# A ternary feed-forward stage with its weights made inside the attention stage before it, and its token tiles written out

## The reference

```python
def _weight_quant(w):
    scale = 1.0 / jnp.clip(jnp.mean(jnp.abs(w)), 1e-05)
    return jnp.clip(jnp.round(w * scale), -1.0, 1.0) / scale

def _act_quant(x):                      # one scale per token
    scale = 127.0 / jnp.clip(jnp.max(jnp.abs(x), axis=-1, keepdims=True), 1e-05)
    return jnp.clip(jnp.round(x * scale), -128.0, 127.0) / scale

def _bitlinear(x, w):
    return jnp.einsum('bsi,oi->bso', _act_quant(x), _weight_quant(w))

gate = silu(_bitlinear(x, w_gate))      # 256 -> 1024
up = _bitlinear(x, w_up)                # 256 -> 1024
y = _bitlinear(gate * up, w_down)       # 1024 -> 256
```

## Time and profile before

| | us |
|---|---|
| median of 3 runs | 4549.73 |
| lowest and highest | 4539.75 and 4550.23 |
| profiled execution | 4542.93 |
| its span, first to last instruction | 4541.1 |

### The profile page before, as it was taken

One profiled execution on the slowest core, in us unless ns is written; L12 is line 12 of the kernel. 1 busy time (PEld: TensorE's weight loads), 2 busy tenths in 40 slices (PEclk: granted clock), 3 DMA queues, 4 the chain that ended last, 5 costly groups with the idle time before them and its releaser, 6 DMA issues. The chain is left out here.

```text
span 4541.1 us, 74932 instructions
## 1 busy us (share of the span) xinstructions
PE 3993.9 (88%) x27065; PEld 2110.3 (46%) x27065; DVE 2500.5 (55%) x3505; ACT 1915.5 (42%) x3522; POOL 1473.1 (32%) x1327
## 2 busy tenths in 40 slices
PE   6667974969999999999999999999999999988564
PEld 4333431635554455445554455435554455435332
DVE  3583444548842688238852588228862588325522
ACT  3344534536532455326542366315643355314321
POOL 0000000026630566116640466106640366200044
PEclk8898996989999999999999999999999999998776
DMA  3000000021120111101120111101120111100386
GB/s 111 28 0 21 0 19 9 2 79 29 28 67 1 32 28 26 57 16 29 28 69 1 28 29 27 58 13 28 29 54 19 25 28 29 61 19 11 97 237 199
DMA packets 103426, 190.31 MB, mean 42 GB/s; under 512 B 14084, under 2 KB 54656, under 8 KB 101888
## 3 DMA queue, kind: packets, MB, share of 16 engines
q1 hardware_dynamic: 94832, 173.21, 13.3%
q0 software_dynamic: 6144, 9.44, 1.1%
q10 hardware_dynamic: 2064, 2.62, 0.2%
HBM read 116.38 MB, written 20.09 MB: 30 GB/s over the span
## 5 line engine op out<-in xcount | busy, mean ns | idle before, releaser
L1510 PE MATMUL PS<-locw,X 128*128 128x512 f32 x2304 | 1109.4, 610 | 81.7 <-issue 42.7
L1777 POOL TENSOR_TENSOR locm<-locm 128x512 f32<-128x512 f32 x384 | 487.7, 1270 | 1004.3 <-DVE locm L1714 1003.9
L1510 PEld LDWEIGHTS PS<-locw,X 128*128 128x128 f32 x2304 | 400.7, 193 | 533.3 <-issue 371.8
L1889 PE MATMUL PS<-locxn,locw 128*114 128x512 f32 (+1 forms) x1152 | 501.4, 593 | 13.0 <-DVE loch L1998 13.0
L1783 POOL TENSOR_TENSOR locm<-locm,locrn 128x512 f32<-128x512 f32 x384 | 392.4, 1043 | 130.2 <-ACT locrn L1629 130.2
L1790 POOL TENSOR_TENSOR locpr<-locpr,locrs 128x512 f32<-128x512 f32 x384 | 391.0, 1039 | 126.2 <-DVE locrs L1743 105.9
L1712 DVE TENSOR_TENSOR locm<-PS,loctab 128x512 f32<-128x512 f32 x384 | 263.5, 686 | 282.0 <-ACT locsq L1619 282.0
L1889 PEld LDWEIGHTS PS<-locxn,locw 128*114 128x114 f32 (+1 forms) x1152 | 204.2, 178 | 306.0 <-issue 282.9
L1654 ACT ACTIVATE locpr<-locpr 128x1024 f32<-128x1024 f32 x192 | 203.1, 1058 | 291.2 <-DVE locpr L1734 291.2
L1650 ACT ACTIVATE locpt<-PS 128x512 f32<-128x512 f32 x384 | 208.4, 595 | 263.2 <-PE PS L1520 263.2
L1998 DVE SCALAR_TENSOR_TENSOR loch<-PS,locvec,locgl 114x512 f32<-114x512 f32 x144 | 107.0, 750 | 376.4 <-PE PS L1889 327.3
(11 more groups left out here) (317 smaller groups left out, 6204.7 us busy)
## 6 DMA issues: line engine op xcount, KB each, us to landing
locve<-locva SPq DMA_DIRECT2D x372, 128.0 KB, 2.2
locw<-in_L2f_wqkv SPq DMA_DIRECT2D x42, 512.0 KB, 9.7
BIG<-in_L3f_gu SPq DMA_DIRECT2D x24, 768.0 KB
BIG<-in_L3f_down SPq DMA_DIRECT2D x24, 384.0 KB
moe_sums<-none SPq DMA_DIRECT2D x2, 4352.0 KB, 23.2
moeroom<-moe_sums SPq DMA_DIRECT2D x16, 512.0 KB, 7.0
locw<-in_L2f_w SPq DMA_DIRECT2D x6, 1364.0 KB
loctab<-in_L2f_tabs SPq DMA_DIRECT2D x7, 1024.0 KB, 10.9
```

The source lines that it names most:

```text
L1510: mm = pe.matmul(PS[:, o % 2, :], k.X[:, j, at - j:at - j + P], W[:, j, col:col + G], start=j == 0, stop=j == KD - 1)
L1777: pool.tensor_tensor(M1[:, j, :], M1[:, j, :], M2[:, x, :], ALU.add).then_inc(s.paired, 1)
L1889: mm = pe.matmul(PS[0:r, 4 + 2 * (m % 2) + half, :], W1[:, c, half * FI + m * FR:half * FI + m * FR + r], XNL[:, g % 2, c, :], start=c == ...
```

## The change

**Weights.** `stage_xattn` takes a triple of hooks, given for L0x alone. SP issues the three 1 MB loads behind the loads of the cross-attention, into unused parts of BIG. DVE does the three sums of absolute values, one each in its steps 3, 4 and 5, and the reciprocal of the means in step 7. POOL, behind its copies, adds the sums over the partitions with an all-reduce, forms the means, and does the nine passes. Five semaphores more belong to L0x. The first block of L0f is gone.

**Tiles.** The 16 tiles are written out, most tiles have two buffers, and XN is read by TensorE directly. x is quantised for two tiles at once, in DVE's odd steps, with the rounding on ACT. gate, up, silu and `hidden` go in two halves of 512 columns. The rounding of h (one pass over 1024 columns) and both products of factors go to POOL; DVE keeps maximum, scale, reciprocal and clipping. The clipping of h comes a step later, its transposes and copy two, the down product three, y's transposes and addition four.

```diff
+def bitnet_weights(k, io):
...
+    WF = [k.BIG[:, KD * T + i * 2048:KD * T + (i + 1) * 2048] for i in range(3)]
...
+    def quantise(pool):
...
+        pool.wait_ge(s.sums, 3)
+        link(pool.partition_all_reduce(k.bit_sum[:, 3:6], k.bit_sum[:, 0:3], P, RSUM))
+        link(pool.tensor_scalar(k.bit_mean[:, :], k.bit_sum[:, 3:6], 1.0 / (D * FF), 1e-5, ALU.mult, ALU.max))
+        pool.sem_inc(s.mean, 1)
+        pool.wait_ge(s.scale, 1)
+        for i in range(3):
+            link(pool.tensor_scalar(WF[i], WF[i], k.bit_scale[:, i:i + 1], ROUND, ALU.mult, ALU.add))
+            link(pool.tensor_scalar(WF[i], WF[i], ROUND, 1.0, ALU.subtract, ALU.min))
+            link(pool.tensor_scalar(k.bit_wq[i], WF[i], -1.0, None, ALU.max))
+
+    def measure(dve, n):
+        if 3 <= n < 6:
+            i = n - 3
+            dve.wait_ge(s.loaded, 48)
+            dve.tensor_reduce(k.bit_sum[:, i:i + 1], WF[i], AX.X, ALU.add, apply_absolute_value=True).then_inc(s.sums, 1)
+        if n == 7:
+            dve.wait_ge(s.mean, 1)
+            dve.reciprocal(k.bit_scale[:, :], k.bit_mean[:, :]).then_inc(s.scale, 1)
...
                 for n in range(NT + 1):
                     if n + 1 < NT:
                         shift(n + 1)
+                    if beside:
+                        beside[2](dve, n)
                     for slot in "AB":
...
+                def gate_up(n, j):
+                    m, i = divmod(n, 2)
+                    pe.wait_ge(s.xqc, m + 1)
+                    if n:
+                        pe.wait_ge(s.h, 2 * (n - 1) + j + 1)
...
+                def turn_y(n):
+                    pe.wait_ge(s.y, n + 1)
...
+                turn_x(0)
+                turn_xq(0)
+                turn_x(1)
+                for n in range(NT + 4):
+                    if n >= 4:
+                        turn_y(n - 4)
+                    if n < NT:
+                        gate_up(n, 0)
+                        gate_up(n, 1)
+                    if 2 <= n < NT + 2:
+                        turn_h(n - 2)
+                    if n % 2 == 0 and n // 2 + 1 < MX:
+                        turn_xq(n // 2 + 1)
+                    if n % 2 and n // 2 + 2 < MX:
+                        turn_x(n // 2 + 2)
+                    if 3 <= n < NT + 3:
+                        down(n - 3)
...
+                def raise_h(n):
+                    pool.wait_ge(s.h_scaled, n + 1)
+                    if n >= 2:
+                        pool.wait_ge(s.hq, n - 1)
+                    pool.tensor_scalar(HR[:, n % 2, :], H[:, n % 2, :, :].rearrange("p j n -> p (j n)"), HS[:, 2, n:n + 1], ROUND,
+                                       ALU.mult, ALU.add).then_inc(s.hr, 1)
+                    pool.tensor_scalar(HS[:, 3, n:n + 1], HS[:, 1, n:n + 1], k.bit_mean[:, 2:3], None, ALU.mult).then_inc(s.h_factor, 1)
...
+                for n in range(NT):
+                    raise_h(n)
+                    if n % 2 and n // 2 + 2 < MX:
+                        factors(n // 2 + 2)
...
+                def raise_x(m):
+                    act.wait_ge(s.x_scaled, m + 1)
+                    if m:
+                        act.wait_ge(s.xq, m)
+                    for i in range(2):
+                        act.activation(XR[:, i, :], PS[:, 4, i * D:(i + 1) * D], ACT.Copy, scale=XS[:, 2, 2 * m + i:2 * m + i + 1],
+                                       bias=ROUND).then_inc(s.xr, 1)
...
+                raise_x(0)
+                copy_xq(0)
+                raise_x(1)
+                for n in range(NT + 3):
+                    if n < NT:
+                        silu(n, 0)
+                        silu(n, 1)
+                    if 2 <= n < NT + 2:
+                        copy_h(n - 2)
+                    if n % 2 == 0 and n // 2 + 1 < MX:
+                        copy_xq(n // 2 + 1)
+                    if n % 2 and n // 2 + 2 < MX:
+                        raise_x(n // 2 + 2)
+                    if n >= 3:
+                        weigh(n - 3)
...
+                def clip_h(n):
+                    dve.wait_ge(s.hr, n + 1)
+                    if n >= 2:
+                        dve.wait_ge(s.hqt, n - 1)
+                    dve.tensor_scalar(HQ[:, n % 2, :], HR[:, n % 2, :], ROUND, 127.0, ALU.subtract, ALU.min).then_inc(s.hq, 1)
...
+                measure_x(0)
+                clip_x(0)
+                measure_x(1)
+                clip_x(1)
+                for n in range(NT + 4):
+                    if n >= 4:
+                        add(n - 4)
+                    if n < NT:
+                        hidden(n, 0)
+                        hidden(n, 1)
+                    if 1 <= n <= NT:
+                        clip_h(n - 1)
+                    if n < NT:
+                        measure_h(n)
+                    if n % 2 and n // 2 + 2 < MX:
+                        measure_x(n // 2 + 2)
+                        clip_x(n // 2 + 2)
```

More of the change, by code:

```diff
@@ new lines, in stage_bitnet_ffn @@
+def stage_bitnet_ffn(nc, k, io):
+    PS, sem = k.PS, k.sem
+    s = Names()
+    (
+        s.xt, s.x_step, s.x_scaled, s.x_factors, s.xr, s.xq, s.xqt, s.xqc, s.gate_ps, s.up_ps, s.silu, s.h, s.h_step, s.h_scaled, s.h_factor,
+        s.hr, s.hq, s.hqt, s.hqc, s.y_ps, s.y, s.yt, s.added
+    ) = (sem("bit_" + n) for n in (
+        "xt", "x_step", "x_scaled", "x_factors", "xr", "xq", "xqt", "xqc", "gate_ps", "up_ps", "silu", "h", "h_step", "h_scaled", "h_factor",
+        "hr", "hq", "hqt", "hqc", "y_ps", "y", "yt", "added"
+    ))
+    NT = T // P
+    MX = NT // 2
@@ L644, in stage_bitnet_ffn @@
-        NT = T // P
-        def steps(eng, step):
-            step(0, 0, False, True)
-            for b, lo, hi in ((0, 1, NT // B + 1), (1, NT // B + 1, NT - 1)):
-                with eng.Fori(lo, hi) as n:
-                    step(n, b, True, True)
-            step(NT - 1, 1, True, False)
+        XS = sb("bitxs", [P, 3, NT])
+        FS = sb("bitfs", [P, NT, 2])
+        XR = sb("bitxr", [P, 2, D])
+        XQ = sb("bitxq", [P, 2, D], BF16)
+        XQT = sb("bitxqT", [P, 2, 2, KD, P], BF16)
@@ new lines, in turn_h, with down @@
+                def turn_h(n):
+                    pe.wait_ge(s.hq, n + 1)
+                    if n:
+                        pe.wait_ge(s.hqc, n)
+                    for c in range(FK):
+                        mm = pe.transpose(PB[:, 6, c * P:(c + 1) * P], HQ[:, n % 2, c * P:(c + 1) * P], k.identb[:, :])
+                    mm.then_inc(s.hqt, 1)
+                def down(n):
+                    pe.wait_ge(s.hqc, n + 1)
+                    if n:
+                        pe.wait_ge(s.added, n)
+                    for c in range(FK):
+                        mm = pe.matmul(PS[:, 7, 0:D], HQT[:, n % 2, c, :], dq[:, c, :], start=c == 0, stop=c == FK - 1)
+                    mm.then_inc(s.y_ps, 1)
@@ L735, in result @@
-                def result(n):
-                    act.wait_ge(hqt, n + 2)
-                    act.activation(HQT[:, :, :], PB[:, 6, :].rearrange("p (c t) -> p c t", c=FK), ACT.Copy).then_inc(hqc, 1)
-                    act.wait_ge(y_ps, n + 1)
-                    act.wait_ge(h_factor, n + 1)
-                    act.activation(Y[:, :], PS[:, 7, 0:D], ACT.Copy, scale=HS[:, 3:4]).then_inc(y_sb, 1)
-                def step(n, b, before, after):
-                    silu(n)
-                    if before:
-                        result(n - 1)
-                    if after:
-                        copy_xq(n + 1)
@@ L749, in _, with copy_xq @@
-                copy_xq(0)
-                steps(act, step)
-                result(NT - 1)
+                def raise_x(m):
+                    act.wait_ge(s.x_scaled, m + 1)
+                    if m:
+                        act.wait_ge(s.xq, m)
+                    for i in range(2):
+                        act.activation(XR[:, i, :], PS[:, 4, i * D:(i + 1) * D], ACT.Copy, scale=XS[:, 2, 2 * m + i:2 * m + i + 1],
+                                       bias=ROUND).then_inc(s.xr, 1)
+                def copy_xq(m):
+                    act.wait_ge(s.xqt, m + 1)
+                    if m >= 2:
+                        act.wait_ge(s.up_ps, 2 * (2 * m - 3) + 2)
+                    act.activation(XQT[:, m % 2, :, :, :].rearrange("p i c t -> p (i c t)"), PB[:, 5, 0:2 * D], ACT.Copy).then_inc(s.xqc, 1)
@@ new lines, in silu, with copy_h @@
+                def silu(n, j):
+                    act.wait_ge(s.gate_ps, 2 * n + j + 1)
+                    act.wait_ge(s.x_factors, n // 2 + 1)
+                    act.activation(GA[:, j, :], PS[:, j, :], ACT.Silu, scale=FS[:, n, 0:1]).then_inc(s.silu, 1)
+                def copy_h(n):
+                    act.wait_ge(s.hqt, n + 1)
+                    if n >= 2:
+                        act.wait_ge(s.y_ps, n - 1)
+                    act.activation(HQT[:, n % 2, :, :], PB[:, 6, :].rearrange("p (c t) -> p c t", c=FK), ACT.Copy).then_inc(s.hqc, 1)
@@ L801, in add @@
-                def add(n, b):
-                    dve.wait_ge(yt, n + 1)
```

(9 more changed lines are left out.)

258 lines of the change are left out of this document (99 added, 159 removed).

## The result

The changed kernel takes 4492.36 us (median of 5, 4490.77 to 4511.65), the kernel before beside it 4539.75 us (5 runs, 4536.73 to 4550.23): ratio 0.9878, 95% interval 0.9858 to 0.9898. A second set, `a1_changed`, gave 4487.6 us (6 runs, 4480.78 to 4497.67) against 4543.12 (17 runs), ratio 0.9876 [0.9854, 0.9898]. The gain is 47 to 56 us. The forecast was 45 and 4505 us, and 4492 lies in its range. The steps behind it did not come out so well.

The account below looks back on a forecast made before the run. It took DVE to bound the tile loop, with the weight phase wholly on the path. A 48 us stage gain less 2.0, 0.5 and 0.4 gave 45, so 4549.7 - 45 = 4505 us, range 4487 to 4520.

Parts of the forecast that it names:

- The weight phase: Between layernorm's end and POOL's first copy: all on the path, so hiding it in L0x removes 31.1 us.
- DVE's own work: Changed tile loop: if nothing else were late, DVE needs 9.1 us per pair of tiles, against 13.0 before.
- The walk of a pair: Steady pair in the tile loop: 12.1 us, 3.0 of it DVE waiting, with ACT-to-TensorE order setting the pace.
- The whole loop: Layernorm's end to last addition: steps sum to 99 us, plus 2 for TensorE's clock, 101 against 148.9.
- A meeting of DVE and POOL: One `normalise` in L0x may meet a POOL pass: 0 to 6.7 us, taken as 0.5.
- L0x, sums: DVE's three sums in L0x steps 3 to 5 delay TensorE: 2.0 us, bounds 0 and 6.9.
- Means in time, passes hidden, rounding 1.0 us: POOL: means by 108 us, before DVE asks; nine passes of 17 us (bound 60) within 63; rounding h 1.0 us.
- The sum: Whole program: 48 us gained in the ternary stage, less 2.0, 0.5 and 0.4, gives a gain of 45 us.
- Rival 1: Tile loop: ACT's and TensorE's order costs nothing, pairs take 9.1 us; gain 60, 4490 us; chance 0.14.
- rival 2: Tile loop: POOL rounds h in 3.4 us, giving back 10; gain 35, 4515 us; chance 0.14.
- rival 3: L0x pays: means late by 5, sums 6.9, blocked `normalise` 4; gain about 32, 4518 us; chance 0.07.
- rival 4: Slower: POOL's rate makes passes outlast L0x and rounding delay even tiles; 4583 us at 6 ns per element; chance 0.02.

Follow-up runs that it names:

- a1_changed: The changed kernel once more, unaltered, timed beside the kernel before: 4487.6 us, ratio 0.9876.
- e1: The kernel before with only the weights moved into L0x on POOL, old tile loop kept: 4496.4 us, ratio 0.9891 to before.
- e5: The changed kernel with y scaled before x is rounded (ACT) and x measured before h (DVE): 4459.4 us, ratio 0.9812 to before.
- e9: The changed kernel with DVE's three sums in L0x over 16 of 2048 columns: 4498.4 us, ratio 0.9893 to before.
- e2: The new tile loop alone, weights made on DVE in a block of their own as before: 4534.3 us, ratio 0.9978 to before.
- e7: The kernel before with 64 tiny unused TensorE products in the weight phase: 4564.3 us, ratio 1.004 to before.
- e3: The changed kernel with ACT's scaling of y put ahead of the rounding of x: 4469.0 us, ratio 0.9832 to before.
- e12: The changed kernel with 6 small unused TensorE products in the ternary stage's start-up: 4493.6 us, ratio 0.9887 to before.
- e6: The kernel before with 12 tiny unused TensorE products in the weight phase: 4528.0 us, ratio 0.9957 to before.

## Why the prediction was right and wrong

- **The weight phase goes, 31.1 us.** Right: the stage's part before the first `hidden` fell from 38.6 to 8.0 us, with e1 28.4 on the whole stage since its old loop ran 2.4 us longer.
- **Start-up 7.5 us.** Right, 8.0 and 7.6.
- **DVE's own work, 9.1 us a pair.** Right, but it shows only in e5 (8.6 to 9.1). In the changed kernel it isn't the bound.
- **The walk of a pair, 12.1 us.** The waits stand where it put them, the pairs take 14.1 to 15.3. Its mistake is in the durations of TensorE, taken from a kernel in which TensorE idled less at a stretch.
- **The whole loop: "so I add 2: 101".** This step failed: the stretch took 113.6. The four full pairs, 48 us in the sum, took 57.9 (from the fifth tile's `hidden` to the thirteenth's), and steps 2 and 3 took 12.6 instead of 9.8. The clock was treated as a surcharge of 2 us carried over from before, when my own walk had TensorE idle for several microseconds in front of `turn_y` in each pair. It should have been asked at which level the products right behind that gap run. By the last steps of the loop, which have no work on x and run at clock 1.00, a tile takes 4.1 us; in the pairs with the gap, which have that work too, 7.1 to 7.6.
- **A meeting of DVE and POOL was priced for L0x alone** (0.5 us, none seen: in all 12 profiles with the hidden passes the `normalise` that ran wholly beside one took 1.22 to 1.23 us, against 1.22, so the 1.9 us by the rule that the prediction names there isn't borne out). It came in the loop, 6 x 0.44 = 2.6 us, on an operation that moves two elements.
- **L0x, sums 2.0 us.** 1.4 by e9 against changed. In 9 of the 12 profiles with the hidden weights the first look at the scores also came later than before's 56.4 us, by 2.7 to 9.5 us. It goes with the clock: from 50 to 55 us it is 0.50 to 0.86 in these nine and 1.00 in the other seven profiles. TensorE waits for the loads for 16 us before, and whether the clock falls in that wait doesn't decide: it stayed at 1.00 there in e2 and e7, which are early, and fell to 0.50 in e3, which is late. Windows from 45 to 60 us of e12, where it had stayed at 1.00 through the wait:

```profile
45.00:50.00 5.00, 5.00 (x30) 4.38 (x30) 1.78 (x2) 0.00 (x0) 0.00 (x0) 0.71 0.00 0
50.00:55.00 5.00, 5.00 (x18) 3.56 (x16) 0.00 (x0) 0.69 (x1) 0.00 (x0) 0.50 0.01 3
55.00:60.00 5.00, 5.00 (x25) 5.00 (x25) 0.00 (x0) 0.00 (x0) 0.00 (x0) 0.50 0.00 0
```

 and of `a1_changed`, the same program up to there, where it had fallen during the wait and was back:

```profile
45.00:50.00 5.00, 5.00 (x36) 4.04 (x35) 0.94 (x2) 0.69 (x1) 0.00 (x0) 1.00 0.00 0
50.00:55.00 5.00, 5.00 (x33) 3.70 (x32) 0.66 (x1) 0.00 (x0) 0.00 (x0) 1.00 0.01 3
```

 The four kernels without the hidden loads had the better case each time (56.0 to 56.4 us). Whether the loads of 3 MB tip it, or four is too few, is open. It matters to the sum: the layernorm ends at 195.6 to 196.2 us in these four, at 196.5 and 196.6 in three with the hidden weights, and at 200.2 to 205.6 in the nine.
- **Means in time, passes hidden, rounding 1.0 us.** Right: 8.3 us, no wait, 1.12 us. The five semaphores cost 0.2 us by the gap behind L0x (1.96 against 1.74), forecast 0.4. The passes' price was wrong by a factor of 2.5, inside the bounds given, and 19 us of room were left. The Trainium skill's rule for one-input work ("GPSIMD Engine Reference", Engine selection), roughly line-rate, holds for two of the four kinds of pass seen.
- **The sum.** By stages the change gives 35.0 in the ternary stage, less 1.8 in L0x (`a1_changed`), about 33 us, where 45 were forecast; with the later layernorm of the nine profiles it would be 26 to 31. The local transformer adds 17.8 to 18.3, a term that the prediction puts at nothing. That these two errors nearly cancel is why the total was near; that is luck, and no merit of the steps. Rival 1 (DVE alone sets the pace) described e5, rival 2's slow rounding and rival 3's late means didn't occur, and nothing came near rival 4. L0x did pay in nine of the twelve profiles, but through the clock, which rival 3 doesn't have.

## What to carry to other kernels

Put the operation that releases TensorE ahead of one that is still waiting for something else in the queue of the engine that makes it: y, ready to be scaled, stood 3.6 us behind a rounding whose input wasn't there. When a walk shows TensorE idle for some microseconds just ahead of work on the path, ask also what the work behind the gap takes at the lower clock, and look for an order that shortens the gap. Two swaps, of operations that cost nothing themselves, were worth 29 us here, four to seven times the tile loop's own rewrite. And before crediting an edit with a total, compare the stages that it doesn't touch: here a third of the gain lay in one of them, and twelve unused products in the kernel before give as much.

## What the runs showed of the hardware

- A `tensor_scalar` on POOL over 128x2048 takes 1.97 us (multiply, add), 1.90 (minimum, maximum), 5.4 (one operation), 7.1 (sum or difference, minimum).
- A DVE `tensor_scalar` of two elements was held for 0.44 us by a POOL instruction that was running, six times of six; POOL's rounding, started while DVE's clipping of x was running, took 1.24 instead of 1.12 us in e5, six times of six. A DVE `tensor_tensor` with two inputs in SBUF ran beside a POOL `tensor_scalar` at its usual 1.22 to 1.23 us in 12 profiles.
- A jump back in TensorE's long loop costs 4.8 to 6.4 us each time, and 2.1 to 4.2 more at most jumps in some programs (before, e2, e7); 48 instructions added elsewhere took that away in e6.
- Around a gap of 4.15 us in TensorE's work the granted clock was 1.00 in the gap and 0.63 in the 3.75 us of products behind it; in e5, where the same wait is at most 0.9 us, it was 0.99 over the loop.
